# Tiles of 128 rows instead of 256 in the two routed stages of a mixture-of-experts kernel

## The reference

```python
logits = xf @ gate_w + gate_b                 # 8 experts
top_w, top_i = jax.lax.top_k(logits, 2)       # two experts for each row
gw = jax.nn.softmax(top_w, axis=-1)
combine = (gw[:, :, None] * one_hot(top_i, 8)).sum(axis=1)
for e in range(8):
    h = gelu(xf @ w1[e] + b1[e])              # 128 -> 512
    out = out + combine[:, e:e + 1] * (h @ w2[e] + b2[e])   # 512 -> 128
shared = gelu(xf @ ws1 + bs1) @ ws2 + bs2     # a ninth expert, for every row
```

## Time and profile before

| | us | share of the span |
|---|---|---|
| median of three runs | 952.41 | |
| the profiled execution | 951.15 | |
| its span, first to last instruction | 949.3 | |
| PE busy | 671.7 | 71% |
| DVE busy | 646.1 | 68% |
| POOL busy | 460.9 | 49% |
| ACT busy | 445.5 | 47% |

### The profile page before, as it was taken

How to read it: one execution, slowest core, us unless ns; L and a number is a source line. 1 busy time by engine, 2 the same in 40 slices (tenths; PEclk the granted TensorE clock), 3 DMA queues, 4 the chain that set the end, 5 groups by cost and what they waited for, 6 DMA issues and landing times. The chain is left out here.

```text
span 949.3 us, 21195 instructions
## 1 busy us (share of the span) xinstructions
PE 671.7 (71%) x7378; PEld 491.6 (52%) x7378; DVE 646.1 (68%) x1459; ACT 445.5 (47%) x873; POOL 460.9 (49%) x569
## 2 busy tenths in 40 slices
PE   0278964860099997157988988888983785999960
PEld 0163433650089996034555655555552464899850
DVE  6989987760278886685666676576661673788865
ACT  6632366730055554355455555455542431555534
POOL 2037758887537777110111226316421784477770
PEclk9978997985589999568999999999997897999995
DMA  9410002241444542521122223213300141454417
GB/s 288 109 35 1 0 7 70 66 88 52 40 73 91 98 92 44 199 57 41 41 66 63 55 63 86 80 52 90 86 8 12 43 80 31 81 96 93 96 32 265
DMA packets 137507, 70.45 MB, mean 74 GB/s; under 512 B 89237, under 2 KB 126619, under 8 KB 137400
## 3 DMA queue, kind: packets, MB, share of 16 engines
q1 hardware_dynamic: 113646, 44.16, 20.7%
q0 software_dynamic: 9088, 16.88, 6.1%
q10 hardware_dynamic: 14672, 8.06, 3.1%
HBM read 26.61 MB, written 30.50 MB: 60 GB/s over the span
## 5 line engine op out<-in xcount | busy, mean ns | idle before, releaser
L2109 DVE TENSOR_REDUCE ARENA<-banks 128x2 f32<-128x512 f32 (+1 forms) x192 | 126.8, 687 | 88.2 <-PE banks L1847 85.7
L1432 ACT ACTIVATE ARENA<-banks,ARENA 128x256 f32<-128x256 f32 x312 | 122.1, 475 | 109.7 <-PE banks L1395 97.6
L1393 PE MATMUL banks<-ARENA,W1H 128*128 128x256 f16 x312 | 87.2, 279 | 69.0 <-DMA ARENA<-slots 62.1
L2031 ACT ACTIVATE ARENA<-banks 128x1536 f32<-128x1536 f32 x64 | 92.0, 1437 | 58.7 <-PE banks L1880 58.7
L1407 PE MATMUL banks<-W2L,ARENA 128*128 x624 | 110.6, 219 | 2.7 <-DVE ARENA L1445 2.3
L1408 PE MATMUL banks<-W2H,ARENA 128*128 x624 | 110.0, 219 | 0.1
L1409 PE MATMUL banks<-W2H,ARENA 128*128 x624 | 110.1, 219 | 0.0
L1383 POOL DMA_INDIRECT expert_out_g<-ARENA x78 | 80.6, 1033 | 47.7 <-issue 25.8
L1383 POOL DMA_INDIRECT expert_out_f<-ARENA x78 | 81.3, 1043 | 39.0 <-issue 25.6
L1466 DVE TENSOR_TENSOR ARENA<-ARENA 128x1024 f16<-128x1024 f32 x78 | 95.6, 1226 | 2.7
L999 POOL DMA_INDIRECT slots<-ARENA,PLACE x64 | 77.3, 1208 | 26.1 <-issue 18.1
(11 more groups left out here) (318 smaller groups left out, 1897.8 us busy)
## 6 DMA issues: line engine op xcount, KB each, us to landing
spread<-ARENA ACTq DMA_DIRECT2D x48, 128.0 KB, 2.0
ARENA<-expert_out_f SPq DMA_DIRECT2D x8, 512.0 KB, 7.2
ARENA<-spread SPq DMA_DIRECT2D x16, 256.0 KB
ARENA<-spread SPq DMA_DIRECT2D x64, 64.0 KB
ARENA<-expert_out_g SPq DMA_DIRECT2D x8, 512.0 KB, 7.2
XT<-in_w SPq DMA_DIRECT2D x10, 256.0 KB, 7.6
slots<-EMPTY SPq DMA_DIRECT2D x16, 129.0 KB, 4.7
ARENA<-in_w SPq DMA_DIRECT2D x8, 256.0 KB, 6.9
```

The source lines that it names most:

```text
L1393: pe.matmul(out, t.W1H[:, e, ms], XST[i][:, 0], start=True, stop=False)
L1432: ins = nc.scalar.activation(HF[i % 2][:, m], UP[i % 2][:, m], ACT.Gelu, bias=BIAS[i % 4][:, m:m + 1], scale=1.0 / WS)
L2031: nc.scalar.activation(PR[G % 2], t.psum_all[:, 5:8, :], ACT.Exp, scale=1.0 / LOGIT).then_inc(exps, 1)
L2109: dve.tensor_reduce(out, src, AX.X, ALU.max).then_inc(m_red, 1)
```

## The change

The number of rows in a tile of the routed stages is one constant:

```diff
-TS = 2 * P
+TS = P
 SLOTS = (2 * NT * P + NE * (TS - 1)) // TS
 ROUNDS = -(-SLOTS // UN)
```

## The result

| | before | after |
|---|---|---|
| median of four runs, us | 952.07 | 1064.08 |
| lowest and highest | 949.72, 954.01 | 1062.89, 1065.18 |
| span of the profiled execution | 949.3 | 1063.4 |
| first routed stage, SP's first transpose to POOL's last scatter starting | 125.75 | 181.0 |
| second routed stage | 121.3 | 177.0 |

The change makes the kernel 1.1179 times as slow, 95% interval 1.1155 to 1.1204. I had forecast 1012, with 957 to 1028 as the range: the direction came out, the size did not. Nearly all of the loss lies in the two routed stages: 55.2 us in the first and 55.7 in the second, where I had given them 27.7 and 32.1. Of the 114.1 us by which the span grew, 3.0 lie between the first stage's last scatter and the second stage's first transpose, where I had put nothing; which work took them was not looked into.

A forecast was written before the change was run, and what follows sets the result against it. SP's queue was to bound the routed stages at 1.95 us per tile; with round changes 6.5, long transposes 3 and a tail of 7.4 us, the stages grew by 27.7 and 32.1, giving 1012 us, range 957 to 1028.

The forecast's parts named there:

- SP's pace: SP's queue in the routed stages: transpose 1.19 us, target rows 0.43, so 1.95 us per tile, slowest of five engines.
- The first rival: Routed stages: the transpose gets cheaper (below 0.8 us) and DVE bounds, 959 us; chance 0.23 including times in between.
- The estimate of 0.53 us: SP's transpose, from the skill page's cycles: SP's pace would be 1.3 us and the time the first rival's.
- The step that failed: PE's work per new tile in the routed stages: 24 matmuls of 128 columns, 1.33 us.
- SP's round changes: SP reads eight registers anew: 0.81 us more each, eight per stage, 6.5 us.
- Long transposes: Some transposes hold SP longer than usual: 3 us per stage, with 0 and 9 as ends.
- DVE: DVE's work per new tile in the routed stages: 1.54 us, bounds 1.36 and 1.65.
- ACT: ACT's four activations of 128 columns per new tile: 1.16 us, below PE.
- The end of the range: Whole kernel: range 957 to 1028 us, leaving out the faster case, the clock and tails of the other two.
- The rival in which PE becomes the bound: Routed stages: gaps drop PE's clock to 1.2 GHz, a tile takes 2.53 us, 1093 us in all; chance 0.04.
- PE at about 75%: Expected sign in the routed stages: PE busy about 75% at a clock of 1.00.
- SP without waits for scatters: Expected sign in the routed stages: SP's transposes 1.95 us apart, without waits for scatters.

The follow-up runs named there:

- Experiment 9: Kernel after, with PE loading one set of eight registers a round instead of two, keeping the first layer's for the second: 1045.79 us, 1.0971.
- experiment 7: Kernel of experiment 6, with both register loads of a round kept but only one of the eight registers used: 984.56 us, 1.0318.
- experiment 1: Kernel after, with PE taking fixed experts from constants, so no register loads or address operations: 1031.2 us, 1.0802.
- experiment 6: Kernel after, with fixed experts on PE and every second transpose left out after the first round: 967.98 us, 1.0165.
- experiment 3: Kernel before, with each first-layer matmul split in two of 128 columns, still 16 register operations per 256 rows: 957.19 us, 1.0037.

## Why the prediction was right or wrong

The time, stepwise, each from a run: the kernel before 952 to 954; tiles of 128 rows with neither PE's addresses nor SP's full queue 968; with SP's full queue 1031; with PE's addresses and one register load a round 1046; with both loads 1064. The steps aren't a sum of costs, since each one is only what stands over the bound below it.

- *SP's pace.* Right: 1.17 us for a transpose of 128 rows (I took 1.19, unchanged, with 0.60 as the other end), 0.43 for the target rows, 1.92 to 1.93 us a tile. The first rival's condition, a transpose below 0.8, is met by none of the 142 (shortest 1.17). The estimate of 0.53 us from the 631 cycles that the Trainium skill gives for generations before the newest ("DMA: Bandwidth & Descriptors", section "Why a DMA increments its semaphore by 16 and not by 1") isn't borne out either; the measurement decides.
- *The step that failed* is PE's: "24 matmuls of 128 columns, 24 x 0.0552 = 1.33 us". It counts matmuls only. Measured were 2.17 us, over SP's 1.95, because 16 register operations a tile stand in the same stream, and half the matmuls no longer cover them. I took the 0.0552 from tiles where these were hidden; the rows of lines 1393 to 1408 with their "PEldq" operations were in the trace of before, with their counts. The same fault is what I did right for SP: I counted there what is paid per tile and not per row. The prediction sized SP's per-tile costs and assumed that PE had none.
- *SP's round changes* (0.81 x 8 = 6.5) were held to be the only ones that count. With PE as the bound its own decide, 1.93 us each, 15 us a stage. Experiment 9 puts some 16 us of the two stages' 31 on one of the two register loads; experiment 7 puts 17 us on both, but in a kernel where PE isn't alone at the bound.
- *Long transposes*, 3 us a stage (0 to 9 in the range): about 8.5, and 10 to 11 with the loads beside them. Twice the surplus makes some 15 of the 19 us by which experiment 1 lies above my 1012. That number was in effect a forecast for the kernel of experiment 1, so the term was mis-sized even there.
- *DVE* at 1.54 (1.36 to 1.65): 1.39 from result to result when free. From the subtract to the result it is 0.68, as worked out, and from the cast to the subtract 0.46 (I had 0.43); the mis-sized term is from the result to the cast, 0.25 and not 0.43. The kernel of experiment 6, at 968, falls within that rival's 947 to 975, but with a shorter pace of DVE and more waiting than the rival had, so that its number came out is partly luck. *ACT* at 1.16: 1.14.
- *The end of the range.* 1028 left no room for a bound that I had not seen. The rival in which PE becomes the bound was there only by its clock. The clock was 0.50 in the first 10 to 13 us of each stage and for some 3.4 us after five of its eight changes of a round, and 1.00 otherwise; what the short stretches cost is within 0.1 us each, so that rival was rightly small. The engine named in it was the right one, for another reason.
- *The signs.* I had written "PE at about 75%". It shows 91%, and I would have read this as a full array. "SP without waits for scatters" was the sign that failed plainly.
- *The direction* wasn't luck alone: with PE's surplus taken away (experiment 1) the bound that I had named still makes the kernel 8% slower. But in the kernel after it is another engine that makes it slower.

## What to carry to other kernels

When a tile is made smaller, list for each engine all that is in its queue once per tile, also the instructions that the profile doesn't count as busy (register operations, register loads), and set them against what they will have to hide behind: here 16 of them hid behind 48 matmul times of 128 columns and not behind 24. Take the pace of PE from start to start and its matmuls in a window, not from the busy share. If weights are picked by a register, do more columns per address, or use each loaded register twice (18 us in experiment 9), before splitting further.

## What the runs showed of the hardware

- Working out a weight's address from a register isn't free on PE: two register operations (46 and 32 ns) in each group of three matmuls of 128 columns stretch the group from 0.166 to about 0.235 us. The same operations cost nothing where every second group has none (experiment 3: 0.0556 us a matmul). That PE's queue works ahead in the others and catches up is my reading for experiment 3; the rows at 905 us of the kernel after show it for a stretch at the lower clock. The remaining 0.3 us of a tile stand mostly at the two changes of layer, where 0.34 us lie between the groups' starts and not 0.24; why isn't told apart, and the profile has them as "issue".
- PE's granted clock fell from 1.00 to 0.50 after ten of sixteen pauses of some 1.7 us without a matmul, for 3.4 us, and this cost the kernel after at most 0.1 us each time, since at the lower level the register operations hide.
- A load of eight registers takes PE 0.59 us and one of sixteen 1.13, about 0.07 us a register.
- A DMA transpose out of DRAM holds SP for 1.17 us at 128 rows and 1.20 at 256, both of 256 columns: within these two shapes the rows hardly matter.
